# A two-layer transformer kernel on one core: contexts of attention heads 0 to 5 regrouped by DMA

## The reference

```python
mod = (_silu(L0_c) @ L0_wmod).reshape(L0_c.shape[0], 6, 1, -1)
h = _layernorm(x, axis=-1) * (1 + ca) + sa
q, k = rope(h @ Wq.T), rope(h @ Wk.T); v = h @ Wv.T      # by heads
scores = jnp.einsum('bhgtd,bhkd->bhgtk', qg, k) / math.sqrt(DH)
scores = jnp.where(causal, scores, jnp.finfo(jnp.float32).min)
attn = jax.nn.softmax(scores, axis=-1)
ctx = jnp.einsum('bhgtk,bhkd->bhgtd', attn, v)
x = x + ga * (ctx.reshape(b, t, E) @ Wo.T)
```

## Time and profile before

| | |
|---|---|
| median of 3 runs | 753.19 us (752.57 to 753.41) |
| the profiled execution: its time | 752.28 us |
| its span, first to last instruction | 750.5 us |
| PE busy | 707.6 us (94% of the span) |
| DVE busy | 480.8 us (64%) |
| ACT, POOL busy | 314.7 us, 313.8 us (42% each) |
| mean granted TensorE clock | 0.991 of full speed |

### The profile page before, as it was taken

One profiled execution on the slowest core, in us unless ns is written; L12 is line 12 of the kernel. 1 busy time (PEld: TensorE's weight loads), 2 busy tenths in 40 slices (PEclk: granted clock), 3 DMA queues, 4 the chain that ended last, 5 costly groups with the idle time before them and its releaser, 6 DMA issues.

```text
span 750.5 us, 10313 instructions
## 1 busy us (share of the span) xinstructions
PE 707.6 (94%) x3718; PEld 429.5 (57%) x3718; DVE 480.8 (64%) x722; ACT 314.7 (42%) x530; POOL 313.8 (42%) x254
## 2 busy tenths in 40 slices
PE   4998899999999998999999999999789999999998
PEld 1444343334333332366778888555357888877886
DVE  3787778788888887439675468768785432337211
ACT  3311367677676667732335211554243323223100
POOL 0325673866665568803366233216422212216300
PEclk9999999999999999999999999999889999999999
DMA  8347516264171100120133100231010111012111
GB/s 301 116 127 223 125 44 166 74 123 72 55 190 35 24 3 2 61 76 23 29 84 98 43 1 0 81 66 48 29 41 0 57 56 56 28 57 63 36 70 43
DMA packets 24111, 53.00 MB, mean 71 GB/s; under 512 B 4252, under 2 KB 8100, under 8 KB 23044
## 3 DMA queue, kind: packets, MB, share of 16 engines
q1 hardware_dynamic: 24068, 52.44, 25.1%
HBM read 45.63 MB, written 6.60 MB: 70 GB/s over the span
## 4 chain that ended last, share of the span: by engine, by line
PE 75%; DVE 14%; issue 5%; POOL 2%; DMA 2%; SPq 1%; ACT 1%; DVEq 0%; POOLq 0%; ACTq 0%
PE ps L895 72%; DVE mxp L1869 3%; DVE st L1711 1%; DMA rq<-in_mask 1%; PE ps L912 1%; DVE xnb L1735 1%; DVE x L1956 1%; DVE x L2069 1%; PE ps L1081 1%; DVE rt L1750 1%; POOL pr L2310 1%; DVE dg L2103 0%; ACT pr L1516 0%; PE ps L1088 0%; DVE qsw L1920 0%
## 5 line engine op out<-in xcount | busy, mean ns | idle before, releaser
L895 PE MATMUL ps<-arena 128*128 128x512 f32 (+1 forms) x1404 | 327.2, 392 | 1.2 <-POOL arena L2416 0.5
L895 PEld LDWEIGHTS ps<-arena 128*128 128x128 f32 (+1 forms) x1404 | 259.9, 186 | 60.8 <-issue 1.7
L1869 DVE TENSOR_REDUCE mxp<-ps 128x2 f32<-128x1024 f32 (+3 forms) x160 | 172.5, 1114 | 40.2 <-PE ps L895 39.6
L1516 ACT ACTIVATE pr<-ps 128x512 f32<-128x512 f32 x288 | 161.3, 597 | 73.7 <-PE ps L895 69.7
L895 PE MATMUL ps<-Kst,Qst 96*128 96x512 bf16 (+3 forms) x384 | 97.0, 330 | 5.4 <-DVE mxp L1869 4.2
L895 PE MATMUL ps<-Qst,Kst 99*128 99x512 bf16 x288 | 96.1, 385 | 1.8 <-ACT pr L1516 1.4
L2310 POOL TENSOR_TENSOR pr<-pr,cap 128x512 int32<-128x512 int32 x56 | 70.2, 1269 | 38.4 <-ACT pr L1516 38.4
L895 PE MATMUL ps<-pr,vr 128*32 128x512 f32 x576 | 76.7, 604 | 1.4 <-POOL pr L2310 1.4
L895 PEld LDWEIGHTS ps<-Kst,Qst 96*128 96x128 bf16 x384 | 35.8, 98 | 50.6 <-DVE mxp L1869 20.9
L895 PEld LDWEIGHTS ps<-Qst,Kst 99*128 99x128 bf16 x288 | 24.6, 97 | 64.3 <-ACT pr L1516 45.8
L2416 POOL TENSOR_TENSOR arena<-raw,arena 128x1024 fp32r<-128x1024 f32 x11 | 26.7, 2431 | 80.1 <-ACT arena L1589 80.1
(11 more groups left out here) (205 smaller groups left out, 842.6 us busy)
## 6 DMA issues: line engine op xcount, KB each, us to landing
wmr<-in_wmr SPq DMA_DIRECT2D x8, 1280.0 KB, 11.1
raw<-in_w SPq DMA_DIRECT2D x16, 512.0 KB, 3.3
Qst<-q_parts SPq DMA_DIRECT2D x42, 128.0 KB
q_parts<-qparts SPq DMA_DIRECT2D x3, 768.0 KB, 4.6
x<-in_x SPq DMA_DIRECT2D x8, 256.0 KB, 5.9
wm<-in_wm SPq DMA_DIRECT2D x4, 512.0 KB, 7.3
raw<-in_up SPq DMA_DIRECT2D x8, 256.0 KB, 2.6
raw<-in_down SPq DMA_DIRECT2D x8, 256.0 KB, 2.5
```

Of the source, the lines that this page charges most:

```text
L895: return nc.tensor.matmul(outp, lhs, rhs, start=start, stop=stop, skip_group_check=True)
L1516: A(pr[:, k % PRING, :], ps[:, t_bank(n, k), :], ACT.Exp, scale=float(DH) ** -0.5).then_inc(exp_done, 1)
L1869: V.tensor_reduce(mxp[:, kh, g0:g0 + heads, i].rearrange("p (b e) -> p b e", e=per), units, AXX, ALU.max)\
```

## The change

**Contexts of heads 0 to 5.** The 8 transposes of `ctx_turn` and DVE's `ctx_norm` go. ACT's copy writes `ot` with the two banks interleaved. SP stores `ot` in DRAM (`ctx_rows`), loads the rows of sums as a 64-partition tile `csum` and the four query heads' rows into `num` with features on partitions, waits for DVE's reciprocals of `csum` (`ctx_invert`, after score unit 18), stores these, waits for the store, and loads them, repeated over 16 partitions each, into `den`. These 11 DMAs (`ctx_dmas(h - 1)`) stand in SP's loop behind the loads of keys and queries of head h + 2. DVE multiplies `num` by `den` once for two heads (`ctx_chunk`; 128 x 1024), in the bodies of heads 3 and 5 and at the start of head 7's. POOL splits the first two of these chunks into `aTr`, DVE the third.

**No turns of att.** The six `att_turn` of head 7 go; the two of the last chunk stay. Heads 6 and 7 keep `ctx_turn` and `ctx_norm`.

**Banks.** From k = 28 in head 6 the transposed units use four banks (4, 5, 1, 3), as those of head 7 did from k = 4 on. Score unit 8 moves from k = 4 to k = 3.

**First loads.** The mask is loaded last, into a tile of its own, and DVE makes its two forms after the first query parts. PE does half of the first values ahead of the first queries.

```diff
-    if h < 2:
-        return h * (NS + 2) + s
-    base = h * (NS + 4) - 4
...
+    return h * (NS + 2) + s
+BY_DMA = NKV - 2
...
-SCORES_AT = (0, 1, 4, 5, 6, 9, 10, 13, 13, 15, 17, 18, 20, 22)
+SCORES_AT = (0, 1, 3, 5, 6, 9, 10, 13, 13, 15, 17, 18, 20, 22)
 CONTEXT_AT = 3
+SUMS_AT = 18
+CHUNK_AT = 8
...
-EARLY_TURNS = [(hf, c) for hf in range(2) for c in range(KC - 1)]
-EARLY_AT = {7 + 4 * k: turn for k, turn in enumerate(EARLY_TURNS)}
+WIDE_AT = 28
@@ def t_bank(n, k):
-    return LAST_T_BANKS[k % 4] if n == LAST else 4 + k % 2
+    wide = n == LAST or n == LAST - 1 and k >= WIDE_AT
+    return LAST_T_BANKS[k % 4] if wide else 4 + k % 2
@@ SP
-            sp.dma_start(rq[0][:, 0:2 * P], a["mask"]).then_inc(mask_in, 16)
             tok = [slice(0, HALF), slice(HALF, T)]
             for hf in range(2):
                 sp.dma_start(cosb[:, tok[hf]], a["cos"][:, tok[hf]]).then_inc(trig_in[hf], 16)
                 sp.dma_start(sinb[:, tok[hf]], a["sin"][:, tok[hf]]).then_inc(trig_in[hf], 16)
+            sp.dma_start(maskf[:, :], a["mask"]).then_inc(mask_in, 16)
...
+            def ctx_dmas(n):
+                half, k = 64 * (n % 2), n // 2 % 2
+                sp.wait_ge(o_copied, 2 * n + 2)
+                sp.dma_start(cscr[n], ot[:, :, :].rearrange("p a b -> p (a b)")).then_inc(ctx_out, 16)
+                if n == 0:
+                    sp.wait_ge(part_q, 3)
+                    sp.wait_ge(q_out, 48)
+                elif n == 4:
+                    sp.wait_ge(at_split, 1)
+                sp.wait_ge(ctx_out, 16 * n + 16)
+                sp.dma_start(csum[:, :, :], cscr[n].rearrange("(s r) (c e) -> r c s e", r=32, e=16)[16]).then_inc(sum_in, 16)
+                for g in range(G):
+                    sp.dma_start(num[k][half + DH * g:half + DH * g + DH, :].rearrange("p (s u) -> p s u", s=4),
+                                 cscr[n].rearrange("(s r) (g u) -> g r s u", r=32, g=G)[g, 0:DH]).then_inc(num_in, 16)
+                sp.wait_ge(inv_ready, n + 1)
+                sp.dma_start(rscr[n].rearrange("s (c e) -> c s e", e=16), csum[:, :, :]).then_inc(inv_out, 16)
+                sp.wait_ge(inv_out, 16 * n + 16)
+                for g in range(G):
+                    sp.dma_start(den[k][half + DH * g:half + DH * g + DH, :].rearrange("p (s u) -> p s u", s=4),
+                                 rscr[n].rearrange("s (g u) -> g s u", g=G)[g].unsqueeze(0)
+                                 .to_broadcast([DH, 4, 2 * P])).then_inc(inv_in, 16)
...
                 if h < 2:
                     store_queries(h + 2)
+                if 0 < h <= BY_DMA:
+                    ctx_dmas(h - 1)
                 if h == WO_LOADED:
@@ PE
             keys(0)
+            values(0, range(2))
             pe.wait_ge(wq_sorted, KC)
             queries(0, 0)
-            values(0)
             ln_turn(0, 1)
+            values(0, range(2, 4))
             keys(1)
...
-                if n == LAST and k >= 4:
+                if n == LAST or n == LAST - 1 and k >= WIDE_AT + 4:
                     pe.wait_ge(exp_done, n * NTU + k - 3)
-                elif k < 2 and n or k >= 2 and n < LAST:
+                elif n == LAST - 1 and k >= WIDE_AT + 2:
+                    pe.wait_ge(s_read, slots_before(LAST, NS))
+                elif n or k >= 2:
                     pe.wait_ge(exp_done, n * NTU + k - 1)
@@ ACT
-                if n:
+                if n == LAST:
                     act.wait_ge(s_full, ctx_at(n - 1) + 2)
+                elif n:
+                    act.wait_ge(ctx_out, 16 * n)
@@ DVE
+            def ctx_invert(n):
+                dve.wait_ge(sum_in, 16 * n + 16)
+                V.reciprocal(csum[:, :, :], csum[:, :, :]).then_inc(inv_ready, 1)
+
+            def ctx_chunk(c):
+                dve.wait_ge(num_in, 128 * c + 128)
+                dve.wait_ge(inv_in, 128 * c + 128)
+                V.tensor_tensor(num[c % 2][:, :], num[c % 2][:, :], den[c % 2][:, :], ALU.mult).then_inc(num_ready, 1)
...
+                    if n and what == "s" and s == SUMS_AT:
+                        ctx_invert(n - 1)
+                    if n in (3, 5) and what == "s" and s == CHUNK_AT:
+                        ctx_chunk(n // 2 - 1)
...
+            ctx_chunk(KC - 2)
+            dve.wait_ge(num_ready, KC - 1)
+            link(V.tensor_copy(aTr[0][:, KC - 2, :], num[0][:, :]))
+            V.tensor_tensor(aTr[1][:, KC - 2, :], num[0][:, :], aTr[0][:, KC - 2, :].bitcast(F32), ALU.subtract).then_inc(at_split, 1)
+            ctx_norm(LAST - 1)
@@ POOL, end of head_pool(n)
+                if n in (3, 5):
+                    c = n // 2 - 1
+                    pool.wait_ge(num_ready, c + 1)
+                    link(tscopy(aTr[0][:, c, :], num[c][:, :]))
+                    nc.gpsimd.tensor_tensor(aTr[1][:, c, :], num[c][:, :], aTr[0][:, c, :].bitcast(F32), ALU.subtract)\
+                        .then_inc(at_split, 1)
```

More of the change, by code:

```diff
@@ L484, in adaln_two_blocks @@
         wsum = at("wsum", [P, MODW], F32, WR_B + 10 * 1024)
-        att = at("att", [P, NT, D], F32, WR_B + 16 * 1024)
+        att = at("att", [P, NT, P], F32, WR_B + 24 * 1024)
+        num = [at(f"num{k}", [P, T], F32, WR_B + (16 + 8 * k) * 1024) for k in range(2)]
+        den = [at(f"den{k}", [P, T], F32, WR_B + (20 + 12 * k) * 1024) for k in range(2)]
+        csum = at("csum", [64, 4, 16], F32, WR_B + 28 * 1024)
         pr = at("pr", [P, PRING, D], F32, HT_B)
@@ L1087, in att_turn @@
                 for t in range(4):
-                    last = nc.tensor.transpose(ps[:, b, tl(t)], att[:, att_slot(4 * hf + t), c * P:(c + 1) * P], ident[:, :])
+                    last = nc.tensor.transpose(ps[:, b, tl(t)], att[:, att_slot(4 * hf + t), :], ident[:, :])
                 last.then_inc(full_b[b], 1)
@@ L1136, in head_body @@
                             max_turn(n + d)
[L1137 removed]
+                        else:
                             mod_step(n + d)
[L1139 to L1140 removed]
             for b in range(4):
                 pe.wait_ge(read_b[b], banks.attn[b])
[L1144 removed]
+            pe.wait_ge(k_ones, 2)
             pe.wait_ge(kst_ones, 1)
@@ L1193, in _ @@
                     if t == 4:
-                        for c in range(KC):
-                            evacuated(pe, ("aT", 1, c))
+                        evacuated(pe, ("aT", 1, KC - 1))
                     b = bank_of(pe, ("wo", t))
                     for kc in range(KC):
-                        last = mm3(ps[:, b, :], hilo(aTr, lambda h: h[:, kc, tl(t)]), hilo(Wo, lambda w: w[:, kc, :]),
+                        at_ = tl(t if kc == KC - 1 else ctx_slot(t))
+                        last = mm3(ps[:, b, :], hilo(aTr, lambda h: h[:, kc, at_]), hilo(Wo, lambda w: w[:, kc, :]),
                                    kc == 0, kc == KC - 1)
@@ L1898, in ctx_norm @@
                     link(V.reciprocal(rec[:, b, :, :], v[:, :, :, 16]))
-                    V.tensor_tensor(att[:, 4 * b:4 * b + 4, n * G * DH:(n + 1) * G * DH]
+                    V.tensor_tensor(att[:, 4 * b:4 * b + 4, (n - BY_DMA) * G * DH:(n - BY_DMA + 1) * G * DH]
                                     .rearrange("p i (g d) -> p g i d", g=G),
@@ L1902, in ctx_norm, with head_body @@
                                     ALU.mult).then_inc(s_read, 1)
-            def head_body(n, nxt, nxt2, ctx):
-                for k, (_, what, d, s) in enumerate(body_steps(nxt, nxt2, ctx)):
+            def ctx_invert(n):
[5 more added lines that the diff above has]
+                V.tensor_tensor(num[c % 2][:, :], num[c % 2][:, :], den[c % 2][:, :], ALU.mult).then_inc(num_ready, 1)
+            def head_body(n, nxt2):
+                for k, (at_, what, d, s) in enumerate(body_steps(True, nxt2)):
                     if n == 0 and k == 2:
```

70 lines of the change are left out of this document (27 added, 43 removed).

## The result

The changed kernel takes 755.93 us (median of 20 runs, 752.8 to 759.1), the kernel before 753.24 (20 runs too, one of them 1020.9 and without weight in the median): a ratio of 1.0036 with a 95% interval of 1.0023 to 1.0048. It is slower by 2.7 us. I had forecast 746.2 and a range from 742.5 to 752.5, with a chance of 0.10 for slower. The profiled execution took 755.34 us for a span of 753.5 us, 3.0 more than the span of before.

The account below looks back on a forecast made before the run. PE was taken as the bound, with three quarters of the chain of waits. Start 1.6, turns 5.2, bodies 2 and 3 -0.4, body 4 -1.1 and head 7 1.7 gave 7.0 gained: 746.2 us, range 742.5 to 752.5.

Parts of the forecast that it names:

- The step that failed: Body 4 into head 5: `wmr` lands at +31.3, rows of maxima at +31.6; PE waits from +29.4, 2.2 us.
- My upper bound of 4.5: Body 4: the loss if the 2.5 MB of `gabc`, `Wo` and `wmr` go at half the rate.
- the 1.07 that I credited for the hidden floor: Body 5: DVE does the floor of `gabc` during PE's wait, so its 1.07 us go.
- the 0.86 of that body: Turns of the context, bodies 1 to 6: 0.86 us gained per body, 5.2 in all.
- The slow rival: Bodies 1 to 5: SP's chain 3 us or more later holds each next body; 759.2 us, chance 0.09.
- a cost of 1.1: Body 4: PE's wait of 2.2 us less the 1.07 of body 5, net 1.1 lost.
- the two waits on ACT: Bodies 1 to 6, between score unit 8 and transposed unit 5: PE waits some 0.4 and 0.26 us for exponentials.
- had slack: DVE per head: 1.5 us of work lost, 0.3 (reciprocal) or 1.2 (chunk) added, taken as covered by slack.
- The rows behind `wmr`: Bodies 2 and 3: rows of maxima come out behind `wmr` at +28.8 to +29.3, costing 0.2 each, 0.4 in all.
- Start: Head 0's scores start at 40.8, not 42.60, as DVE no longer stands for the mask; 1.6 gained, bounds 0.9 and 2.2.
- The push: Head 7: DVE's three chunk operations delay POOL's `Wo` splits and masks by 2.7 us, bounds 0 and 3.6; 1.7 still gained.
- the forecast 7.0: Whole kernel: net gain of 1.6 + 5.2 - 0.4 - 1.1 + 1.7 = 7.0 us.

Follow-up runs that it names:

- the swap: Changed kernel with the rows of maxima issued ahead of the `wmr` load in each body: 745.78 us, ratio 0.9922 to the kernel before.
- the start alone: Kernel before with only the changed kernel's load order, late mask in its own tile and half of first values ahead of first queries: 750.90 us, ratio 0.9976.
- the kernel with two banks: Changed kernel with rows of maxima ahead of `wmr` and two banks instead of four for head 6's late units: 746.15 us, ratio 0.9912.
- both edits: Changed kernel with rows of maxima ahead of `wmr` and the reciprocal of the sums after score unit 17, not 18: 746.98 us, ratio 0.9914.
- the earlier reciprocal: Changed kernel with DVE's reciprocal of the sums after score unit 16, not 18: 748.42 us, ratio 0.9944 to the kernel before.

## Why the prediction was wrong, point by point

**The step that failed** is, in the words of the prediction, "`wmr` +31.3, and the rows of maxima of head 5 at +31.6. PE waits for them from +29.4: 2.2 us". The rows landed at +37.8 and PE waited 8.07. The mechanism was right (the swap shows it) and the term was mis-sized. I took the time of 2.25 MB from the difference of two landings, `gabc` and `wmr`, 5.5 us. While `gabc` was landing, the others behind it were already moving, so the difference leaves out what lay beside it: in the trace of before DMA moved only 1.39 MB from 221.3 to 227, of the 2,304 KB issued behind `gabc`. The whole group was in the same rows: from the issue of `gabc` at 212.80 to the landing of `wmr` at 226.8 are 14.0 us. Put after +23.0 that gives +37.0, 0.8 from the truth. That it comes so near is in part luck: those 14.0 had query loads ahead and none behind, the 15.1 of the changed kernel the other way round. My upper bound of 4.5 was taken from the same difference, and wrongly: at half the rate the 5.5 become 11.0, so the wait is 7.7 and the net loss 6.6. Worked out rightly, the bound would have come near the wait of 8.07.

The rows are 6.2 us later than I had them: 4.1 are bytes (12.7 against the 8.6 that I had from `gabc` to the rows), 2.4 the key and query loads issued behind the rows (each good to about 1 us, as said above), and SP's start, 0.2 earlier, goes the other way (the rest is rounding). Together with it came a cost that the sum did not have at all: after 8 us idle PE ran at the lower clock for a while (0.63 over 4.73 us), 1.66 us in head 5's body. So the 1.07 that I credited for the hidden floor and the 0.86 of that body did not show: it takes 31.39, as before.

**The slow rival** (0.09, 759.2) named the right place but another cause and another price: SP late by 3 us or more. SP was on time. What came was slower, by a way that was in my sum as a cost of 1.1.

**Bodies.** At unit 5 the gain is what I had. The product round after it starts 0.93 us earlier in its body than before, of 0.86 forecast. Of the two waits on ACT one is written out (0.26); the other lies inside the pair of units 4 and 5, which takes 0.88 where such a pair takes 0.60. But 0.34 of it goes at the turn of the maxima, where PE waits for `nm` in every body. DVE's reciprocal stands ahead of the last maximum (body 2, DVE's timeline):

```profile
164.46 0.54 DVE L1942 RECIPROCAL csum<-csum 64x64 f32<-64x64 f32 x1
164.92 1.16 DVE L1906 TENSOR_REDUCE mxp<-ps 128x2 f32<-128x1024 f32 x1
166.11 0.19 DVE L1912 TENSOR_TENSOR nm<-mxp 128x32 f32<-128x32 f32 x1
```

I had put this reciprocal at 0.3 us without a row for it; it takes 0.54. And I had written that DVE "had slack". It has, over a body, but not at the one place where PE stands next behind it. A body is 0.53 shorter. The rows behind `wmr` cost 0 in body 2 and 0.42 in body 3, where I had 0.2 each.

**Start.** Head 0's first score stands at 40.67 (40.8 forecast), head 1's body begins 1.80 earlier (1.6), and the start alone brought 1.6. Right.

**Head 7.** The push was right: POOL's splits took 2.6 us longer beside DVE's three operations (2.7 forecast). From unit 0 of head 7 to the turn of its context the gain was 0.27, and head 6 with its late rows gained 1.2; of 2.56 for the two, 1.5 came. Its late rows are DVE's small operations beside the splits, which I had seen in one row (the 1.26 of the earlier trace rows) and charged only to POOL. They took the same in the kernel before, where PE came later and found the rows there.

**The sum in the spans**: start 1.80 gained, bodies 1 to 3 1.10, body 4 7.61 lost, body 5 0.07 lost, body 6 1.21, head 7 0.27 and the rest 0.3 gained: 3.0 lost. With the forecast 7.0 gained, 10.0 are missing, and 8.3 of them are body 4 (6.3) and body 5 (2.0).

What stays open: why 2.5 MB and the rows behind them need 12.7 us when a `wmr` alone lands in 5.3. Whether other sizes of transfer would do it sooner was not tried.

## What to carry to other kernels

When a change moves an issue in a queue, ask what small, urgent transfer now stands behind large ones, and take the time of the whole group from the first issue to the last landing, never from a difference of landings. If the small one is urgent, issue it first: it cost the large ones nothing here (`wmr` landed 13.5 us after the issue of `gabc`, 14.3 in the changed kernel). And slack of an engine is not an average: look at which instruction of it the bound engine waits for next, and put new work behind that one.

## What the runs showed of the hardware

- Small rows issued behind 2.5 MB landed 7.8, 8.5 and 11.7 us after their issue. By these figures two of the three landed before `wmr`, which was issued ahead of them (near 238.4 and 240.0, against 243.1), and the third, for which PE waits, after it. Without the loads issued after them the last row and `wmr` landed over 2 us sooner, so order in the queue does not shield a transfer from what is issued behind it. The prediction quoted the Trainium skill (DMA: Bandwidth & Descriptors, Queues, rings and completion order) for rings consumed in order, and took from it that nothing passes `wmr`. That goes further than the section, which also says that a later descriptor may finish its write before an earlier one; the trace agrees with the section, as two rows did pass. The price of 2.4 for what stands behind is measured here alone, in one pair of profiles.
- The prediction also quoted the Trainium skill (DMA: Bandwidth & Descriptors, Anatomy of one DMA — SWDGE (gpsimd) path) for a fixed 2.0 us per DMA. The section is on DMAs that GpSimd issues, and these are issued by SP; here the stores of inverse sums landed in 2.0 to 3.4 us, the one in body 4 in 2.0.
- A wait of 8.07 us brought the granted clock of the next 4.7 us to 0.63, one of 5.66 to 0.50 and one of 2.18 to 0.64, the first and the last at 1.66 and 1.1 us of lost time. Waits of 0.91 and, in the kernel with two banks, 1.40 at the same place cost nothing: both bodies took 29.7. A wait of 1.82 in head 7 left the next product round at 1.07 us in one profile (the swap) and at 1.57 in another (both edits), so the length of the wait alone does not settle it.
- DVE and POOL operations from SBUF to SBUF delay each other. A `nm` of 128 x 32 in head 0's body took from 0.19 to 2.05 us in the profiles of these kernels, whatever the edit, by where it met POOL's operations of 128 x 1024 on the query parts; PE waited up to 1.79 for it. The other way round, POOL's copy of 128 x 512 took 1.91 us beside DVE's `num` of 128 x 1024, and 0.62 alone. In head 0 the clock varies too: after the same waits of 0.87, 0.25 and 1.38 us the granted clock from 82 to 92 us was 1.00 in four profiles (the swap and the earlier reciprocal among them) and 0.66 to 0.83 in all others, the kernel before included. Both may be a part of the spread of 5 us between the runs of one kernel; no run isolates them.
